# A graph network on one core: where POOL's matrix writes stand, and how deep its gathers run ahead

## The chip, the core and the metric

The kernel runs on one core of one Trainium2 chip. The metric is the device time of one execution in microseconds (us). TensorE (PE, with its weight loads as PEld), VectorE (DVE), ScalarE (ACT), GpSimd (POOL) and SyncE (SP) run their own instruction streams and meet by semaphores. POOL issues all indirect DMAs here: those that read rows of a table by a list of indices, or write elements to places that a list gives.

## The reference

The reference is a chain of eight blocks on x, 1875 nodes x 256 features, each added to x. Four have to do with the change. The first is a stack of four graph layers over 31875 edges sorted by destination:

```
e = edge_attr @ eW + eb
m = relu(x[src] + e)
agg = segment_sum(m, dst, num_segments=N)
h = (1.0 + eps) * x + agg
return relu(h @ W1 + b1) @ W2 + b2
```

with `y = relu(layernorm(h))` between layers. Then comes a feed-forward block on the half of the nodes with the highest score. The third is relational attention with 8 relations and 8 heads:

```
h_all = einsum('nf,rof->rno', x, W)
scores = einsum('ehd,hd->eh', h_all[edge_type, src], attn_src) + einsum('ehd,hd->eh', h_all[edge_type, dst], attn_dst)
scores = leaky_relu(scores);  w = exp(scores - amax[dst]);  w = w / denom[dst]
out = segment_sum(h_src * w, dst)
```

Behind it stand a switch feed-forward block, a two-layer graph convolution (which uses the edge weights as a dense matrix), a top-2 block, another convolution and a last top-2 block.

## The kernel before

The nodes are held as T = 15 tiles of 128 rows, the edges as EC = 264 chunks of 128. A loop pass handles U = 12 chunks in groups of G = 4, so there are 264 / 12 = 22 passes. The program is cut into phases; at the end of each, all engines meet in a barrier, so a phase lasts as long as its slowest engine.

**The matrix writes.** The convolutions behind the attention want the edge weights as dense adjacency matrices in HBM. `Adjacency.send(pool, count)` writes the next `count` of the 264 chunks, 128 single elements each, as one indirect DMA (L488). Nothing needs them before the first convolution, where `arrived` waits for all. So the kernel hands them to POOL in small lots in phases in which POOL has little else to do: 4 in each of four dense parts (`gine_mlp`), 6 in each of three norms between the layers, 10 in the stack's last norm, 30 in the ranking of the nodes, 6 in the attention's norm, 14 in `relation_scores`, and the remaining 170 at the start of `relation_rows`.

**The edge stage** (`gine_edges`, four times). For each chunk POOL gathers the source rows from an HBM table into one of RING = 24 buffers (`gather_rows`, L833), TensorE makes the edge term (L880, L881), VectorE adds it (L919), ScalarE applies relu (L898), TensorE sums by destination with a one-hot matrix (L890), and VectorE adds the sum to the accumulator (L927). The buffer is free when `agg_done` counts the chunk; `gather_rows` knows this semaphore as `used`.

**The norm** (`layernorm`) computes on VectorE, writes the gather table through SP, and turns the tiles on TensorE (L676) for the next stage.

**The rows stage** (`relation_rows`, phase "score"). In each pass VectorE makes 12 one-hot tiles and raises `hot_ready` after each group of four (L1992), TensorE turns them (L1930), ScalarE copies them out (L1964), TensorE picks the destination scores (L1940), and VectorE multiplies and reduces (L1999, L2003). The first T = 15 passes also compute the rows of the relation table (L1919), which ScalarE copies (L1972) and SP writes to HBM; the last 7 passes have no such products. POOL has no part in it but the matrix writes.

**The ordered attention** (`attend_in_order`, phase "inorder"). POOL gathers rows of 264 values from that table into HELD = 44 buffers (L2219). Windows of up to 11 chunks go through a chain of small operations on VectorE and TensorE (L2276 to L2299) before their messages are weighted and summed as in the edge stage.

Of the kernel before, what the change touches and what calls it, by code (L numbers as in the profile page):

```python
# [22 lines left out]
EC = 264  # L23
# [6 lines left out]
G = 4  # L30
# [795 lines left out]
def gather_rows(nc, pool, rows, table, got, gathered, used):  # L826


    for c in range(EC):

        if c >= RING:
            pool.wait_ge(used, c - RING + 1)
        pool.indirect_dma_start(got[:, c % RING, :], None, table,  # L833
                                bass.IndirectOffsetOnAxis(ap=rows[:, c:c + 1], axis=0)).then_inc(gathered[c % RING], 16)
# [96 lines left out]
def gine_mlp(nc, g, agg, h, w1, b1, w2, b2, first, stats):  # L931


    with Phase(nc, "mlp") as ph:
# [17 lines left out]
        @block.gpsimd  # L952
        def _(pool):
            g.adj.send(pool, 4)

# [55 lines left out]
def gine_stack(nc, g, i):  # L1011

    with Phase(nc, "stack") as ph:
# [3 lines left out]
        for k in range(L):  # L1017
            table = g.dram(f"gine_table{k}", [NP, D])
            affine = {} if k == 0 else dict(gamma=i["L0_gnn_gamma"][k, :], beta=i["L0_gnn_beta"][k, :], relu=True, stats=stats, edges=6)
            layernorm(nc, g, g.X if k == 0 else h, y, table=table, addrow=i["L0_gnn_eb"][k, :], turned=acc,  # L1020
# [3 lines left out]
                     i["L0_gnn_b2"][k, :], first=(k == 0), stats=stats)  # L1024
        layernorm(nc, g, h, y, gamma=i["L0_gnn_gamma"][0, :], beta=i["L0_gnn_beta"][0, :], relu=True, add=g.X, stats=stats, edges=10)

# [10 lines left out]
def rank_tokens(nc, g, xn, wr, br, chosen, r):  # L1037
# [4 lines left out]
    with Phase(nc, "rank") as ph:  # L1042
# [19 lines left out]
        @block.gpsimd  # L1062
        def _(pool):
            g.adj.send(pool, 30)

# [664 lines left out]
def relation_scores(nc, g, xt, w, attn_src, attn_dst, score_src, score_dst, o):  # L1730
# [5 lines left out]
    with Phase(nc, "rel") as ph:  # L1736
# [31 lines left out]
        def _(pool):  # L1768
            nc.gpsimd.iota(chunk[:, :], [[1, EC + PADS]], base=0, channel_multiplier=0,
                           allow_small_or_imprecise_dtypes=True).then_inc(chunk_made, 1)  # L1770
            g.adj.send(pool, 14)

# [86 lines left out]
def relation_rows(nc, g, score_src, score_dst, scores, xt, wt, h_table):  # L1859
# [4 lines left out]
    with Phase(nc, "score") as ph:  # L1864
# [35 lines left out]
        def _(pool):  # L1900
            nc.gpsimd.iota(rel_idx[:, :], [[1, R]], base=0, channel_multiplier=0,
                           allow_small_or_imprecise_dtypes=True).then_inc(iota_made, 1)
            g.adj.send(pool, 170)

# [282 lines left out]
def attend_in_order(nc, g, o, h_table, scores, acc):  # L2187
# [6 lines left out]
    with Phase(nc, "inorder") as ph:  # L2194
# [19 lines left out]
        def _(pool):  # L2214
            for c in range(EC):

                if c >= HELD:
                    pool.wait_ge(agg_done, c - HELD + 1)
                pool.indirect_dma_start(got[:, c % HELD, 0:FULL], None, h_table,  # L2219
                                        bass.IndirectOffsetOnAxis(ap=g.hrow[:, c:c + 1], axis=0)).then_inc(gathered[c % HELD], 16)  # L2220
# [146 lines left out]
def relational_attention(nc, g, i):  # L2367

    h_table = g.dram("h_table", [NP * R, FULL])
    with Phase(nc, "rgat") as ph:  # L2370
        scores, order = ph.sb("scores", [P, EC, HD]), Order(ph.sb)
        with Phase(nc, "rgat_in") as inner:
            score_src, score_dst = inner.sb("score_src", [P, T, R, HD]), inner.sb("score_dst", [P, T, R * HD])
            xt = inner.sb("xt", [P, T, 2, P])
            with Phase(nc, "rgat_ln") as first:
                xn = first.sb("xn", [P, T, D])
                layernorm(nc, g, g.X, xn, turned=xt, edges=6)
            relation_scores(nc, g, xt, i["L1_gnn_W"], i["L1_gnn_attn_src"], i["L1_gnn_attn_dst"], score_src, score_dst, order)
# [109 lines left out]
```

## Time and profile before

| | us |
|---|---|
| median of 3 runs | 4837.89 (4830.57 to 4844.03) |
| the profiled execution | 4816.76 |
| its span | 4815.1 |
| edge stages, each | 411 to 413 |
| rows stage (2349.5 to 2833.6) | 484.0 |
| ordered attention (2833.6 to 3269.6) | 436.0 |
| POOL busy, in all | 1824.1 (38%) |
| TensorE busy, in all | 2940.5 (61%) |
| VectorE busy, in all | 2290.0 (48%) |

The stage times are from the first instruction of a phase on VectorE to the next phase's. Busy shares of the whole span mix phases with different limits, so a phase is read by itself: which engines are busy in it, and what ends last. A gap between two instructions is put down to a releaser. "issue" means that the engine waited for nothing that the profile shows. Semaphore names are reused, so a releaser such as "DMA unpack_rows<-in_edge_rows" in a late phase stands for another semaphore in the same slot.

### The profile page before, as it was taken

To read this page: it belongs to the slowest core of one execution; us is meant where nothing else is said; L and a number is where in the kernel's file an instruction comes from. 1 tells how busy PE (TensorE), PEld (TensorE's weight loads), DVE (VectorE), ACT (ScalarE), POOL (GpSimd) and SP (SyncE) were. 2 spreads that over 40 slices of the span, in tenths; PEclk is the share of its full clock that TensorE was granted. 3 is DMA by queue.
4 is the path that set the end of the run, shared out by engine and by line. 5 is a ranking of instruction groups with operands and counts; after the bars stand their busy time and mean duration, and the time that the engine had idled before them with its cause. 6 is when DMAs were issued, how large, how long until landed. Compare 5 with 4: busy or idle time off the path is not lost. (4 is left out here: it accounts for less than half of the span.)

```text
span 4815.1 us, 58214 instructions
## 1 busy us (share of the span) xinstructions
PE 2940.5 (61%) x16851; PEld 2371.2 (49%) x16852; DVE 2290.0 (48%) x6653; ACT 868.0 (18%) x2228; POOL 1824.1 (38%) x1982
## 2 busy tenths in 40 slices
PE   3566756675667566606405945673949829948392
PEld 3455545554555455405304723333948729937382
DVE  7666556665665566652202436784154421134113
ACT  1122212221222222202001310000310103310020
POOL 4366446645663566342472036651010020020212
PEclk8788878887888788857557956775979959979696
DMA  6633223322332333215001213332947539945594
GB/s 163 207 90 91 69 76 89 90 62 84 90 90 53 91 90 90 48 37 181 18 1 46 89 45 89 95 71 81 335 156 240 186 103 331 327 161 171 176 334 133
DMA packets 357404, 599.03 MB, mean 124 GB/s; under 512 B 81862, under 2 KB 239864, under 8 KB 354808
## 3 DMA queue, kind: packets, MB, share of 16 engines
q1 hardware_dynamic: 245816, 357.76, 22.2%
q0 software_dynamic: 88640, 214.25, 15.6%
q10 hardware_dynamic: 22656, 23.54, 1.5%
q8 instruction: 132, 2.16, 0.2%
q14 instruction: 160, 1.31, 0.1%
HBM read 499.63 MB, written 95.75 MB: 124 GB/s over the span
## 5 line engine op out<-in xcount | busy, mean ns | idle before, releaser
L833 POOL DMA_INDIRECT gine_got<-gine_table,src x1056 | 1003.6, 950 | 672.7 <-issue 269.2
L890 PE MATMUL gine_p_sum<-gine_hot,gine_got 128*128 128x128 f32 x4224 | 843.9, 332 | 537.7 <-issue 209.6
L890 PEld LDWEIGHTS gine_p_sum<-gine_hot,gine_got 128*128 128x128 f32 x4224 | 690.3, 232 | 731.1 <-issue 622.3
L919 DVE TENSOR_TENSOR gine_got<-gine_got,gine_p_edge 128x256 f32<-128x256 f32 x1056 | 440.3, 417 | 563.2 <-PE gine_p_edge L881 336.8
L898 ACT ACTIVATE gine_got<-gine_got 128x256 f32<-128x256 f32 x1056 | 439.8, 416 | 1182.2 <-issue 690.4
L927 DVE TENSOR_TENSOR stack_acc<-stack_acc,gine_p_sum 128x256 f32 x1056 | 437.7, 415 | 3.5
L2219 POOL DMA_INDIRECT edge_space<-h_table,hrow x264 | 262.6, 995 | 386.1 <-issue 329.9
L488 POOL DMA_INDIRECT adjacency<-value,place x264 | 264.7, 1002 | 311.9 <-POOLq L54 133.9
L842 DVE TENSOR_SCALAR gine_hot<-iota_free,dst 128x128 f32<-128x128 f32 x1056 | 348.8, 330 | 60.2 <-issue 29.2
L880 PE MATMUL gine_p_edge<-gine_w_a,edge_space 128*128 128x256 bf16 x1056 | 331.7, 314 | 34.7 <-DVEq L910 17.4
L1365 PE MATMUL ffn_p_h<-ffn_xt,ffn_w 128*128 128x128 f32 x2864 | 347.5, 279 | 0.9 <-DMA ffn_w<-in_L_ffn_w 0.4
L1365 PEld LDWEIGHTS ffn_p_h<-ffn_xt,ffn_w 128*128 128x128 f32 x2864 | 337.6, 196 | 2.9 <-DMA ffn_w<-in_L_ffn_w 1.8
L1377 PE MATMUL ffn_p_y<-ffn_w,ffn_ht 128*128 128x256 f32 x1432 | 328.6, 380 | 5.4 <-DMA ffn_w<-in_L_ffn_w 5.3
L881 PE MATMUL gine_p_edge<-gine_w_b,edge_space 128*128 128x256 bf16 x1056 | 331.0, 313 | 0.0
L2254 PE MATMUL inorder_p_sum<-edge_space,inorder_hot 128*128 128x265 f32 x528 | 235.8, 562 | 133.5 <-issue 70.0
L1431 DVE TENSOR_TENSOR ffn_y<-ffn_p_y,ffn_b 128x256 f32<-128x256 f32 x112 | 47.6, 425 | 549.3 <-PE ffn_p_y L1377 549.3
L1402 ACT ACTIVATE ffn_ht<-ffn_p_h,ffn_b 128x128 f32<-128x128 f32 x716 | 204.7, 369 | 549.1 <-PE ffn_p_h L1365 549.0
L1630 PE MATMUL gcn_p_out<-gcn_h,gcn_a 128*128 128x256 f32 x1350 | 299.0, 380 | 0.0
L1377 PEld LDWEIGHTS ffn_p_y<-ffn_w,ffn_ht 128*128 128x128 f32 x1432 | 263.7, 190 | 39.2 <-DMA ffn_w<-in_L_ffn_w 7.7
L1630 PEld LDWEIGHTS gcn_p_out<-gcn_h,gcn_a 128*128 128x128 f32 x1350 | 254.2, 191 | 33.0
L2254 PEld LDWEIGHTS inorder_p_sum<-edge_space,inorder_hot 128*128 128x128 f32 x528 | 108.2, 253 | 229.6 <-issue 227.6
L1143 POOL IOTA route_e_idx<- 128x8 f32 (+1 forms) x3 | 0.4, 136 | 573.9 <-POOLq L54 573.9
(398 smaller groups left out, 3537.1 us busy)
## 6 DMA issues: line engine op xcount, KB each, us to landing
gcn_a<-adjacency SPq DMA_DIRECT2D x270, 320.0 KB
ffn_w<-in_L_ffn_W SPq DMA_DIRECT2D x74, 1024.0 KB
ffn_w<-in_L_ffn_w SPq DMA_DIRECT2D x60, 1024.0 KB
ffn_w<-in_L_ffn_w SPq DMA_DIRECT2D x90, 512.0 KB
adjacency<-zero_row ACTq DMA_DIRECT2D x3, 7200.0 KB, 43.7
gine_got<-gine_table,src POOLq DMA_INDIRECT x1056
h_table<-score_rows SPq DMA_DIRECT2D x15, 1056.0 KB
adjacency<-zero_row SPq DMA_DIRECT2D x1, 7200.0 KB, 28.1
```

The lines of the kernel that those rows point to most:

```text
L833: pool.indirect_dma_start(got[:, c % RING, :], None, table, bass.IndirectOffsetOnAxis(ap=rows[:, c:c + 1], axis=0)).then_inc(gathered[c % ...
L842: nc.vector.tensor_scalar(hot[:, c % HOTS, :], g.iota_free[:, :], g.dst[:, c:c + 1], None, ALU.is_equal).then_inc(hot_ready, 1)
L880: nc.tensor.matmul(p_edge[c % 4][:, 0:D], g.attrs_t[:, c, :], w_a[:, :], start=True, stop=False)
L881: nc.tensor.matmul(p_edge[c % 4][:, 0:D], g.attrs_t[:, c, :], w_b[:, :], start=False, stop=True).then_inc(edge_done, 1)
L890: ins = nc.tensor.matmul(p_sum[d % 4][:, half * P:(half + 1) * P], got[:, d % RING, half * P:(half + 1) * P], hot[:, d % HOTS, :], start=T ...
L898: nc.scalar.activation(got[:, c % RING, :], got[:, c % RING, :], ACT.Relu).then_inc(msg_ready, 1)
L919: nc.vector.tensor_tensor(got[:, c % RING, :], got[:, c % RING, :], p_edge[c % 4][:, 0:D], ALU.add).then_inc(summed, 1)
L927: nc.vector.tensor_tensor(a, a, p_sum[d % 4][:, 0:D], ALU.add).then_inc(added, 1)
L1365: ins = nc.tensor.matmul(p_h[n % 2][m // 4][:, m % 4, :], w1_sb[:, n % 2, k, m * P:(m + 1) * P], xt[:, n % 2, k, :], start=(k == 0), stop= ...
L1377: ins = nc.tensor.matmul(p_y[n % 2][:, 0:D], ht[:, n % 2, m, :], w2_sb[:, n % 2, m, :], start=(m == 0), stop=(m == m_all - 1))
L1630: ins = nc.tensor.matmul(p_out[d][:, 0:D], a[:, n % RA, d * P:(d + 1) * P], h[:, t, :], start=(t == 0), stop=(t == T - 1))
L2254: nc.tensor.matmul(p_sum[c % SUMS][:, 0:WIDE], hot[:, c % HOTS, :], got[:, c % HELD, :], start=True, stop=True).then_inc(agg_done, 1)
```

## The change

Three things change, all of them on POOL. The matrix writes are spread otherwise:

| phase | before | after |
|---|---|---|
| four dense parts | 4 each | 0 |
| three norms between layers | 6 each | 17 each |
| last norm of the stack | 10 | 20 |
| ranking | 30 | 45 |
| norm of the attention | 6 | 12 |
| relation scores | 14 | 4 |
| rows stage | 170 at its start | 132, two after each `hot_ready` |

In the rows stage POOL waits before each pair of writes until VectorE has finished the next group's one-hot tiles. `gather_rows` may be only `min(24, 4 + c // 2)` chunks ahead, which is 24 from chunk 40 on. And of the first 44 gathers of the ordered attention only two are in flight at a time.

```diff
@@ gather_rows
-        if c >= RING:
-            pool.wait_ge(used, c - RING + 1)
+        ahead = min(RING, 4 + c // 2)
+        if c >= ahead:
+            pool.wait_ge(used, c - ahead + 1)
         pool.indirect_dma_start(got[:, c % RING, :], None, table,
@@ gine_mlp
-            g.adj.send(pool, 4)
+            g.adj.send(pool, 0)
@@ gine_stack
-            affine = {} if k == 0 else dict(..., edges=6)
+            affine = {} if k == 0 else dict(..., edges=17)
...
-        layernorm(nc, g, h, y, ..., add=g.X, stats=stats, edges=10)
+        layernorm(nc, g, h, y, ..., add=g.X, stats=stats, edges=20)
@@ ranking
-            g.adj.send(pool, 30)
+            g.adj.send(pool, 45)
@@ relation_scores
-            g.adj.send(pool, 14)
+            g.adj.send(pool, 4)
@@ relation_rows
-            g.adj.send(pool, 170)
+            for n in range(EC // G):
+                pool.wait_ge(hot_ready, n + 1)
+                g.adj.send(pool, 2)
@@ attend_in_order
                 if c >= HELD:
                     pool.wait_ge(agg_done, c - HELD + 1)
+                elif c >= 2:
+                    pool.wait_ge(gathered[c - 2], 16)
@@ relational_attention
-                layernorm(nc, g, g.X, xn, turned=xt, edges=6)
+                layernorm(nc, g, g.X, xn, turned=xt, edges=12)
```

What this does to POOL's instruction stream is seen at three places. (The names in brackets are those of semaphores that first had the slot; a wait "for unpack6_moved1_5" is one for `agg_done` or `hot_ready` of the phase.)

The first is POOL from the second dense part through the norm into the third edge stage. Before:

```order
L952 UNCONDITIONAL_BRANCH [waits barrier_Pool_Activation_PE_DVE_SP_gather]
L488 DMA adjacency<-value,place 3720192x1 x4
L54 UNCONDITIONAL_BRANCH
L723 UNCONDITIONAL_BRANCH [waits barrier_Pool_Activation_PE_DVE_SP_gather]
L488 DMA adjacency<-value,place 3720192x1 x6
L54 UNCONDITIONAL_BRANCH
L868 UNCONDITIONAL_BRANCH [waits barrier_Pool_Activation_PE_DVE_SP_gather]
L833 DMA gine_got<-gine_table,src 128x256 x24
L833 DMA gine_got<-gine_table,src 128x256 [waits gine10_gathered11] x240
```

After:

```order
L953 UNCONDITIONAL_BRANCH [waits barrier_Pool_Activation_PE_DVE_SP_gather]
L723 UNCONDITIONAL_BRANCH [waits barrier_Pool_Activation_PE_DVE_SP_gather]
L488 DMA adjacency<-value,place 3720192x1 x17
L54 UNCONDITIONAL_BRANCH
L869 UNCONDITIONAL_BRANCH [waits barrier_Pool_Activation_PE_DVE_SP_gather]
L834 DMA gine_got<-gine_table,src 128x256 x7
L834 DMA gine_got<-gine_table,src 128x256 [waits gine10_gathered11] x257
```

The dense part's writes are gone, the norm's are 17, and of the 264 gathers 7 instead of 24 go without a wait.

The second is POOL in the rows stage. Before:

```order
L1899 UNCONDITIONAL_BRANCH [waits barrier_Pool_Activation_PE_DVE_SP_gather]
L1901 IOTA score_rel_idx 128x8
L488 DMA adjacency<-value,place 3720192x1 x170
L54 UNCONDITIONAL_BRANCH
L63 ISA [waits barrier_Pool_Activation_PE_DVE_SP_gather]
```

After, the first two pairs of 66:

```order
L1900 UNCONDITIONAL_BRANCH [waits barrier_Pool_Activation_PE_DVE_SP_gather]
L1902 IOTA score_rel_idx 128x8
L488 DMA adjacency<-value,place 3720192x1 [waits unpack6_moved1_5]
L488 DMA adjacency<-value,place 3720192x1
L488 DMA adjacency<-value,place 3720192x1 [waits unpack6_moved1_5]
L488 DMA adjacency<-value,place 3720192x1
```

Where 170 writes stood without any wait, each pair now waits for VectorE.

The third is POOL in the ordered attention. Before:

```order
L2213 UNCONDITIONAL_BRANCH
L2219 DMA edge_space<-h_table,hrow 128x264 x44
L2219 DMA edge_space<-h_table,hrow 128x264 [waits unpack6_moved2_4] x220
L54 UNCONDITIONAL_BRANCH
L2392 UNCONDITIONAL_BRANCH [waits barrier_Pool_Activation_PE_DVE_SP_gather]
```

After, with the first waits and the last of 42:

```order
L2216 UNCONDITIONAL_BRANCH
L2224 DMA edge_space<-h_table,hrow 128x264 x2
L2224 DMA edge_space<-h_table,hrow 128x264 [waits pairs7_spread]
L2224 DMA edge_space<-h_table,hrow 128x264 [waits pairs7_compared]
L2224 DMA edge_space<-h_table,hrow 128x264 [waits pairs7_summed]
...
L2224 DMA edge_space<-h_table,hrow 128x264 [waits gine10_msg_ready]
L2224 DMA edge_space<-h_table,hrow 128x264 [waits unpack6_moved2_4] x220
L54 UNCONDITIONAL_BRANCH
```

Each of gathers 2 to 43 now waits for the landing of the gather two before it.

## Rows read from the trace of the kernel before

**Rows 1.** Windows by stage: a gather stage, rank, the rows stage in two halves; columns in the first row.

```profile
core 0: us, PE busy (x) PEld busy (x) DVE busy (x) ACT busy (x) POOL busy (x), PEclk, DMA share, GB/s
645.00:1057.00 412.00, 266.49 (x1604) 210.32 (x1602) 246.19 (x804) 112.43 (x267) 251.05 (x264) 0.84 0.31 86
2064.00:2137.00 73.00, 0.40 (x1) 0.10 (x1) 54.12 (x112) 0.00 (x0) 32.05 (x30) 0.50 0.08 16
2350.00:2592.00 242.00, 35.32 (x149) 22.77 (x150) 16.15 (x41) 7.86 (x16) 165.82 (x171) 0.53 0.07 14
2592.00:2833.00 241.00, 208.37 (x1389) 159.46 (x1387) 115.68 (x381) 67.27 (x140) 0.00 (x0) 0.80 0.15 63
```

**Rows 2.** Timeline of TensorE in the rows stage (start us, us, engine, line, op [idle before <-releaser]).

```profile
2359.89 1.44 PE L1930 MATMUL score_p_hot<-ident_b,score_hot 128*128 128x128 bf16 x12 [17.52 <-issue]
...
2366.05 0.72 PE L1940 MATMUL score_p_dst<-score_parts,edge_space 128*128 x19
...
2402.58 0.59 PE L1919 MATMUL score_p_rows<-score_wt,score_x_tile 128*128 128x256 f32 x1 [2.21 <-issue]
```

**Rows 3.** Timeline of VectorE in the rows stage: two products of matmul results.

```profile
2414.51 0.42 DVE L1999 TENSOR_TENSOR score_picked<-score_p_dst,score_rel 128x256 f32<-128x256 f32 x1 [56.68 <-DMA unpack_rows<-in_edge_rows]
...
2588.97 0.42 DVE L1999 TENSOR_TENSOR score_picked<-score_p_dst,score_rel 128x256 f32<-128x256 f32 x1 [97.63 <-DMA unpack_rows<-in_edge_rows]
```

**Rows 4.** Timeline of POOL in the rows stage: its last matrix write.

```profile
2568.33 0.97 POOL L488 DMA_INDIRECT adjacency<-value,place  x1 [0.30 <-issue]
```

**Rows 5.** Timeline of VectorE at the start of the second gather stage: chunks 4 and 7.

```profile
660.96 0.42 DVE L919 TENSOR_TENSOR gine_got<-gine_got,gine_p_edge 128x256 f32<-128x256 f32 x1 [0.47 <-issue]
...
687.90 0.42 DVE L919 TENSOR_TENSOR gine_got<-gine_got,gine_p_edge 128x256 f32<-128x256 f32 x1 [10.95 <-DMA unpack_rows<-in_edge_rows]
```

**Rows 6.** Timeline of POOL in the second gather stage: gathers 0 and 28, a burst, the last.

```profile
649.94 0.98 POOL L833 DMA_INDIRECT gine_got<-gine_table,src  x1 [20.75 <-POOLq L54]
...
689.60 0.94 POOL L833 DMA_INDIRECT gine_got<-gine_table,src  x1 [3.31 <-DMA unpack_rows<-in_edge_rows]
...
881.60 0.95 POOL L833 DMA_INDIRECT gine_got<-gine_table,src  x1 [1.21 <-DMA unpack_rows<-in_edge_rows]
...
890.43 0.95 POOL L833 DMA_INDIRECT gine_got<-gine_table,src  x1 [1.62 <-DMA unpack_rows<-in_edge_rows]
...
1035.03 0.94 POOL L833 DMA_INDIRECT gine_got<-gine_table,src  x1 [0.58 <-PE gine_p_sum L890]
```

**Rows 7.** Windows of single passes of the rows loop: one with products, one without.

```profile
2604.00:2617.00 13.00, 12.29 (x82) 9.88 (x81) 5.50 (x20) 4.16 (x9) 0.00 (x0) 0.89 0.20 83
2768.00:2779.00 11.00, 7.26 (x48) 4.73 (x48) 5.76 (x19) 1.76 (x3) 0.00 (x0) 0.50 0.00 0
```

**Rows 8.** Timeline of POOL in the ordered attention: gather 11.

```profile
2852.65 0.95 POOL L2219 DMA_INDIRECT edge_space<-h_table,hrow  x1 [0.30 <-issue]
```

**Rows 9.** Timeline of VectorE in the ordered attention: a score window and two stalls.

```profile
2855.57 0.25 DVE L2276 TENSOR_TENSOR inorder_score<-rgat_scores,edge_space 128x88 f32<-128x88 f32 x1 [12.50 <-DMA edge_space<-h_table,hrow]
...
2887.61 0.16 DVE L2290 TENSOR_TENSOR inorder_carry<-inorder_p_carry,rgat_joined 96x2 f32<-96x2 f32 x1 [13.15 <-DMA gine_table<-ln_rows]
...
2910.03 0.26 DVE L2299 TENSOR_TENSOR inorder_less<-inorder_score,inorder_p_back 128x96 f32<-128x96 f32 x1 [14.61 <-remote]
```

**Rows 10.** Timeline of POOL before the third gather stage: its first gather.

```profile
1119.77 0.99 POOL L833 DMA_INDIRECT gine_got<-gine_table,src  x1 [19.81 <-POOLq L54]
```

**Rows 11.** Timeline of POOL in the final norm: the seventh matrix write of ten.

```profile
2042.97 1.54 POOL L488 DMA_INDIRECT adjacency<-value,place  x1 [0.30 <-issue]
```

**Rows 12.** Timeline of VectorE in the final norm: its last operation.

```profile
2054.25 0.96 DVE L777 SCALAR_TENSOR_TENSOR X<-stack_y,X 128x768 f32<-128x768 f32 x1
```

**Rows 13.** Timeline of TensorE in the relation scores: tiny matmuls, and what follows them.

```profile
2287.84 0.31 PE L1783 MATMUL rel_p_near<-ident,rel_spread 128*96 128x1 f32 x2
2288.01 0.31 PE L1784 MATMUL rel_p_near<-ident,rel_spread 128*96 128x1 f32 x2
...
2305.97 13.81 PE L1791 MATMUL rel_p_proj<-rel_heads,rel_w 128*128 128x16 f32 x64
```

More of the change, by code:

```diff
@@ L1018, in gine_stack @@
             table = g.dram(f"gine_table{k}", [NP, D])
-            affine = {} if k == 0 else dict(gamma=i["L0_gnn_gamma"][k, :], beta=i["L0_gnn_beta"][k, :], relu=True, stats=stats, edges=6)
+            affine = {} if k == 0 else dict(gamma=i["L0_gnn_gamma"][k, :], beta=i["L0_gnn_beta"][k, :], relu=True, stats=stats, edges=17)
             layernorm(nc, g, g.X if k == 0 else h, y, table=table, addrow=i["L0_gnn_eb"][k, :], turned=acc,
@@ L1024, in gine_stack @@
                      i["L0_gnn_b2"][k, :], first=(k == 0), stats=stats)
-        layernorm(nc, g, h, y, gamma=i["L0_gnn_gamma"][0, :], beta=i["L0_gnn_beta"][0, :], relu=True, add=g.X, stats=stats, edges=10)
+        layernorm(nc, g, h, y, gamma=i["L0_gnn_gamma"][0, :], beta=i["L0_gnn_beta"][0, :], relu=True, add=g.X, stats=stats, edges=20)
 class Routes:
```

## The prediction

> **What bounds the kernel now.** I read the windows stage by stage first [rows 1]. A gather stage of the first part, 412 us, has POOL busy 251 us in 264 indirect DMAs (264 x 0.95); with the 0.30 us gap behind each, POOL is taken for about 330 of 412 us. The stage that makes the score rows shows something else: 242 us in which TensorE does 149 matmuls while POOL does 170 writes, then 241 us in which POOL does nothing and TensorE does 1389. Two of the 22 passes of its loop end in the first half, twenty in the second.
>
> The timelines say why. The stage's first matmul starts at 2359.89, and seven microseconds of matmuls run at full pace, up to 2366.8, though POOL has been writing since the stage began [rows 2]. From there TensorE starts about one matmul in 2.8 us (0.59 busy, 2.21 idle, "issue": nothing that the profile shows holds it). VectorE idles 56.68 and 97.63 us ahead of its products of matmul results [rows 3], though the first twelve L1940 matmuls for it had been issued by 2366.8. The stall ends with POOL's last write at 2568.33 + 0.97 = 2569.3 [rows 4], and 23 us later the second pass is done. So **POOL issuing indirect DMAs back to back starves TensorE's issue and holds back its completion signals**; how it does so the trace doesn't show. A write takes POOL 0.97 us and the gap of 0.30 behind the one before it: 1.27 apart [rows 4].
>
> The same pattern, weaker, is in the gather stage. From 649.9 POOL issues without a wait; VectorE adds chunk 4 at 660.96 and is only at chunk 7 by 687.90, with 10.95 us of idle ahead of it [rows 5]. POOL, 24 buffers ahead, waits 3.31 us at 689.60; later it issues six from 881.60 on and pauses 1.62 us, 8.83 us for six chunks [rows 6].
>
> **The change part by part.** The sum is made against the profiled execution, 4816.8 us (span 4815.1); the median of the runs shown is 4837.9, 21 above it.
>
> *Rows stage.* 170 writes at once become 6 per pass: two after each `hot_ready`. hot_ready comes 1.3 us apart at the start of a pass, so the six writes go out as one burst of 6 x 1.27 = 7.6 us, and then POOL waits for the next pass. Behind POOL's new waits stand only its own later writes, and nobody waits for those before the dense stages, so none of POOL's work is on the path if a pass is longer than 7.6 us. Undisturbed, a pass with products takes about 12.5 us (PE busy 12.29 of the 13.00 us of one), one without about 11.0 [rows 7]. What a burst costs in a pass is not in the trace. Bounds: nothing, as the first 7 us of the stage ran at full pace beside POOL [rows 2]; at most the whole burst, 7.6 us. Nearest row: in the gather stage six issues and a pause take 8.83 us [rows 6], where TensorE's 266.5 us for 264 chunks [rows 1] are 1.01 each, 6.1 for six: a burst of the same length costs 2.7 us there. I take 2.6 for the 15 passes with products and 1.0 for the 7 short ones, where TensorE has slack (7.3 busy of 11 us). Start to first matmul is 10.4 us. Sum: 10.4 + 15 x (12.5 + 2.6) + 7 x (11.0 + 1.0) = 321 us for 484: **-163**. With nothing lost 10.4 + 188 + 77 = 275: -209. With 7.6 lost in each long pass and 5 in the short: 10.4 + 302 + 112 = 424: -60.
>
> *Gather stages, four of them.* `ahead` is 7 at chunk 6, grows by one for two chunks, and is 24 from chunk 40. POOL stops early, so TensorE's signals flow earlier, and the gap of VectorE from 661 to 688 should vanish. But what ends the stage is POOL: its last gather, at 1035.03 [rows 6], needs chunk 240 used, and then 22 us drain a full ring of 24. Gather 40 needs 17 chunks used, before and after. Before, gather 28 is issued at 689.60, 40 us behind the first, and twelve more at 8.83 / 6 make 57; POOL alone would need 40 x 1.25 = 50. The pauses only come earlier. I take 0; bounds from -7 (no pause up to 40) to +5 a stage.
>
> *Ordered attention.* The first 44 gathers go two in flight. Gather 11 is issued at 2852.65 [rows 8] and the score sum that needs it starts at 2855.57 [rows 9]: 2.9 us from issue to use, so two in flight give one per 1.5 us instead of 1.25: 44 x 0.25 = +11, and the second score window starts later. Against it the stalls that VectorE has there now, 13.15 and 14.61 us [rows 9], shrink. From there the ring of 44 rules as before. Net +3, bounds -30 (both stalls given back in full) to +11.
>
> *Writes moved into the normalizations.* A gine stage's norm had six writes, then POOL idled 19.81 us before the first gather at 1119.77 [rows 10]. The six had begun at 1092.3 (1100.0 less 6 x 1.28). Seventeen take 17 x 1.28 = 21.8 us, to 1114; beside VectorE operations with two SBUF inputs one takes 1.54 instead of 0.97 [rows 11], which makes about 1118, just inside the stage's end near 1119. Those writes now lie beside the norm's last transposes on TensorE (L676) too, whose signals may be late: +2 each, +6 for three; up to +8 each. The Trainium skill ("SBUF — State Buffer", section "Who interferes with whom") says that a VectorE instruction with two SBUF inputs contends with a GpSimd instruction that reads SBUF; the 1.54 beside 0.97 agrees in kind, and by the page the writes beside one-input operations stay at 0.97, which is the 1114 above.
> The final norm gets 20 for 10: it ends at 2055.2 with VectorE [rows 12]. Its seventh write ends at 2044.5 [rows 11]; thirteen more at 1.27 to 1.84, mostly the former, end at 2061 to 2068: **+9** (6 to 13), since the stage's barrier waits for POOL. Rank, 45 for 30, has 73 us, VectorE busy for most of it [rows 1], and at 32.05 / 30 + 0.30 = 1.37 the 45 need 62: 0 (uncovered, +21). The norm before the relations, 12 for 6: +2 (0 to 7.7, six writes uncovered). The four dense parts lose 4 writes each, 5 us of POOL, shorter than the 16 us before the first hole above: 0 (-1 each).
>
> *Relation scores.* 104 tiny matmuls take 2287.5 to 2305.97 = 18.4 us; at first two start every 0.17 [rows 13], which makes 8.8 for all. The first four of the fourteen writes end ahead of them all: -10, and the 13.81 us matmuls behind, too, may gain a little: **-12** (-8 to -17).
>
> Sum: -163 + 0 + 3 + 6 + 9 + 2 - 12 = **-155**: 4662 for the profiled execution, 4683 for the median.
>
> **The rivals.**
> (1) *A burst blocks a whole pass* (0.17). Twelve L1940 results took from 2366.8 to 2414.5 to reach VectorE; if every signal of a burst is held until POOL pauses, a long pass is 20 us: -60 for the stage, -52 in all, 4786; half of it, 17.5, gives 10 + 263 + 96 = 369, -115 + 8: 4731. For: the late results [rows 3]. Against: the gather stage's 8.83 us, where signals pass within bursts [rows 6], and a stall that began only after some 16 us of POOL [rows 2].
> (2) *A pass hides the burst* (0.17): -209 + 8: 4637. For: the full pace at first [rows 2]. Against: the 8.83 us [rows 6].
> (3) *The shallow rings pay* (0.15). If the 20 to 25 us that VectorE loses at the start of each gather stage are not given back, four stages give -80 and ordered attention -25 more: 4578. For: those stalls are real [rows 5, 9]. Against: POOL's 330 us of issue and its pauses remain, and the drain of a full ring.
> (4) *TensorE was never held by POOL* (0.03), the other sign. Then its 2.8 us a matmul is something of the loop itself, passes stay as they are, and the writes hang behind them: rows 484, plus 9 + 6 + 2 + 3 - 0: 4858. It decides where a pass with six writes takes over 22 us (22 x 22 = 484). Against: 149 matmuls before POOL's last write and 1389 behind it, in equal time [rows 1]. The Trainium skill's section named above says that TensorE and ScalarE never wait on anyone; by it this rival would hold, and the trace disagrees with it as far as issue and signals go.
>
> **How the numbers follow.** My forecast has 0.48: 4683, its own range 4650 to 4710. The cases around it span 4578 to 4786; leaving out the far ends of (1) and (3) gives 4590 to 4765. A measurement here tells 0.3%, 14 us, from no change. Faster by over 0.3% are all cases but (4) and part of the worst of (1): 0.96; within 0.3% 0.015; slower 0.025.
>
> **What would show it.** Rows stage: passes of even length near 15 us from the first on, POOL's writes in 22 groups of six; no idle of VectorE over 10 us. A pass of 12.5 shows (2), of 20 (1). Gather stages: 411 us again with POOL's first wait at chunk 7. Final norm 9 us longer, ended by POOL; L1783 and L1784 without holes. The prediction is wrong if a pass differs from 15 by more than 3 us, or if a gather stage moves by more than 6.

## The result, and the profile after

The changed kernel takes 4702.94 us (median of 4 runs, 4693.92 to 4704.62) against 4837.82 us (4 runs) of the kernel before: a ratio of 0.9718, 95% interval 0.9700 to 0.9736. The prediction was 4683, with a range of 4590 to 4765. The page of the changed kernel begins with its span and the busy time of each engine:

```profile
span 4701.8 us, 58214 instructions
...
PE 2962.1 (63%) x16851; PEld 2391.2 (51%) x16852; DVE 2289.9 (49%) x6653; ACT 868.4 (18%) x2228; POOL 1835.2 (39%) x1982
```

TensorE and POOL are busy for about as long as before; it is their place that changed. The same windows as in [rows 1, 7], now of the changed kernel: a gather stage, the rows stage, a pass with products and one without, the ordered attention.

```profile
core 0: us, PE busy (x) PEld busy (x) DVE busy (x) ACT busy (x) POOL busy (x), PEclk, DMA share, GB/s
650.00:1068.00 418.00, 270.88 (x1596) 214.53 (x1596) 246.85 (x804) 112.75 (x267) 252.86 (x267) 0.82 0.31 85
2384.00:2707.00 323.00, 249.48 (x1536) 188.96 (x1536) 131.52 (x422) 76.03 (x156) 127.86 (x133) 0.74 0.21 57
2420.00:2435.00 15.00, 13.56 (x81) 10.62 (x81) 5.77 (x19) 4.26 (x9) 5.82 (x6) 0.84 0.19 73
2624.00:2636.00 12.00, 7.32 (x49) 4.70 (x49) 5.76 (x19) 1.76 (x3) 3.87 (x4) 0.53 0.01 0
2707.00:3156.00 449.00, 261.16 (x734) 132.23 (x734) 296.08 (x1029) 10.87 (x53) 263.98 (x264) 0.70 0.31 80
```

The rows stage is one stretch of 323 us where [rows 1] had 242 and 241, and its 1536 matmuls are spread over all of it. The gather stage and the ordered attention are a little longer than before. Two timelines of the stage show one pass (start us, us, engine, line, op [idle before <-releaser]). First POOL, with one burst of six and the start of the next:

```profile
2407.24 0.96 POOL L488 DMA_INDIRECT adjacency<-value,place  x1 [9.36 <-DVE score_hot L1995]
...
2413.60 0.97 POOL L488 DMA_INDIRECT adjacency<-value,place  x1 [0.31 <-issue]
2421.76 0.97 POOL L488 DMA_INDIRECT adjacency<-value,place  x1 [7.19 <-DVE score_hot L1995]
```

Then VectorE in the same pass, from its first operation (L1989) to that of the next pass:

```profile
2405.87 0.26 DVE L1989 TENSOR_TENSOR score_rel<-score_rel_idx,etype 128x96 f32<-128x96 f32 x1 [0.47 <-issue]
...
2416.11 0.42 DVE L2002 TENSOR_TENSOR score_picked<-score_p_dst,score_rel 128x256 f32<-128x256 f32 x1 [7.58 <-DMA unpack_rows<-in_edge_rows]
...
2420.39 0.26 DVE L1989 TENSOR_TENSOR score_rel<-score_rel_idx,etype 128x96 f32<-128x96 f32 x1 [0.45 <-issue]
```

A pass is 14.52 us here. POOL's burst begins 1.4 us into it and ends at 2413.60 + 0.97 = 2414.57; the product of matmul results comes 1.5 us behind that, and 4.3 us later the pass is over. The idle of 56.68 and 97.63 us of [rows 3] is gone; what is left is 7.58 in this pass. The releaser in the product's row, a DMA, is the profile's guess. The 15 passes with products take 14.5 to 16.8 us, 15.1 on average, the one behind them 14.3, and the last six 12.0 to 13.2.

The two profiled executions differ by 113 us (4816.8 to 4703.4), the medians by 135. So I ran both kernels again on one chip (below); there their spans are 4813.3 and 4678.1, 135.2 apart. Stage lengths in us, counted from VectorE's arrival at the end of one stage to its arrival at the end of the next, so that the wait at a late barrier counts for the stage behind it:

| stage | before, again | after, again | difference | predicted |
|---|---|---|---|---|
| four gather stages | 1645.1 | 1653.7 | +8.6 | 0, and +6 for the norms |
| final norm with what stands behind it, rank | 105.1 | 116.1 | +11.0 | +9 |
| relation scores, with the attention norm's end | 82.3 | 80.6 | −1.7 | −12 + 2 |
| rows stage | 485.9 | 320.5 | −165.4 | −163 |
| ordered attention | 439.1 | 450.4 | +11.3 | +3 |
| sum | | | −136.2 | −155 |

Counted from barrier to barrier instead, the four gather stages moved by 0.4 us together and the norms ahead of them by 8.5, of which 5.9 are the norm before the third gather stage, whose barrier is late. The rows stage is then 485.8 and 324.3 us, the attention 439.1 and 446.5: 4 us of the attention's +11.3 are the late barrier behind the rows stage. The dense parts and all else moved by 1.0 us together. In the first pair of profiles, 113 us apart, the rows stage gave 160.5 us and the four gather stages with their norms took 27 of it back.

### The profile page after: what moved, and what is told of

Same layout as the page of the kernel before. It is cut to its first block and busy times, and to the rows that moved or that the text cites. A ratio compares the mean times of both kernels' runs of the same rounds, so it can differ in the third digit from the quotient of the medians.

```text
span 4701.8 us, 58214 instructions
## 1 busy us (share of the span) xinstructions
PE 2962.1 (63%) x16851; PEld 2391.2 (51%) x16852; DVE 2289.9 (49%) x6653; ACT 868.4 (18%) x2228; POOL 1835.2 (39%) x1982
## 5 line engine op out<-in xcount | busy, mean ns | idle before, releaser
L891 PE MATMUL gine_p_sum<-gine_hot,gine_got 128*128 128x128 f32 x4224 | 857.1, 336 | 539.2 <-ACT gine_got L899 250.8
L891 PEld LDWEIGHTS gine_p_sum<-gine_hot,gine_got 128*128 128x128 f32 x4224 | 703.3, 236 | 734.8 <-issue 641.6
L488 POOL DMA_INDIRECT adjacency<-value,place x264 | 278.9, 1056 | 478.5 <-POOLq L54 171.4
L928 DVE TENSOR_TENSOR stack_acc<-stack_acc,gine_p_sum 128x256 f32 x1056 | 440.1, 417 | 3.4
```

The lines of the kernel that those rows point to most:

```text
L891: ins = nc.tensor.matmul(p_sum[d % 4][:, half * P:(half + 1) * P], got[:, d % RING, half * P:(half + 1) * P], hot[:, d % HOTS, :], start=T ...
L928: nc.vector.tensor_tensor(a, a, p_sum[d % 4][:, 0:D], ALU.add).then_inc(added, 1)
```

## The experiments

**One part of the change at a time** (four kernels, one chip). `rows_alone` is the kernel before with only the rows stage's writes paced:

```
-            g.adj.send(pool, 170)
+            for n in range(EC // G):
+                pool.wait_ge(hot_ready, n + 1)
+                g.adj.send(pool, 3 if n < 38 else 2)
```

> The kernel before with the rows stage's 170 writes paced (three after each of the first 38 hot_ready, two after the rest) and nothing else changed. Theory (POOL's back to back writes starve TensorE in this stage alone): the rows stage falls from 484 to about 325, since a long pass takes about 15 us; passes with nine writes (11.4 us of POOL) may be longer, up to 17.5. Whole kernel 145 to 160 us below before. Rival (the gain needs the redistribution too, since 170 writes don't fit): the stage stays above 370.

`old_rings` is the changed kernel with the gather rings of the kernel before:

```
-        ahead = min(RING, 4 + c // 2)
-        if c >= ahead:
-            pool.wait_ge(used, c - ahead + 1)
+        if c >= RING:
+            pool.wait_ge(used, c - RING + 1)
```

> The changed kernel with gather_rows as before (24 ahead from the start). Theory (the shallow start costs each gather stage 5 us): the four stages return from 417, 418, 422, 417 to 411 to 413 us (the third to 416, where 5 us are a late barrier of the norm), the kernel is 20 to 22 us faster than the changed one. Rival (the 5 us come from the writes that now stand ahead of the stage): the stages keep their 417, no difference.

`old_attention` is the changed kernel with the ordered attention's gathers unpaced, and `writes_only` has both edits, so that of the change only the moved writes are left:

```
-                elif c >= 2:
-                    pool.wait_ge(gathered[c - 2], 16)
```

> The changed kernel with the ordered attention's gathers as before (44 without a wait). Theory (two in flight cost 1.55 instead of 1.25 us each and win nothing): the stage returns from 449 to 436, the kernel 13 us faster than the changed one. Rival (the stage is longer for another reason, such as its tables' place or the stage before): 449 stays.

> The changed kernel with both rings as before, so that only the matrix writes are redistributed. If the costs add: 20 to 22 and 13 us, 33 to 35 below the changed kernel, about 4668 us. If gather stages and attention hold the same loss for another reason: the changed kernel's 4703.

Measured: the kernel before took 4285.15 us on this chip (13 runs, 4276 to 4292), over 500 less than elsewhere. Against it `rows_alone` took 4299.03 (1.0033, 1.0021 to 1.0045), `old_rings` 4325.01 (1.0082, 1.0066 to 1.0099), `old_attention` 4319.31 (1.0081, 1.0064 to 1.0098) and `writes_only` 4308.61 (1.0050, 1.0033 to 1.0067). All my numbers missed, since what the change removes wasn't there: this chip didn't hold TensorE. POOL's waits in the first gather stage of `writes_only` (waited for: us in total, times, longest):

```profile
POOL gine_got L833 <- POOLq L54: 74.0, 1, 74.0
POOL gine_got L833 <- issue: 66.4, 218, 0.3
POOL gine_got L833 <- PE gine_p_sum L890: 13.7, 45, 0.3
```

No wait is over 0.3 us but the first, which is a barrier, and a gather stage takes 344 us. On the chip of the next group POOL did wait; the changed kernel there, same view:

```profile
POOL gine_got L834 <- POOLq L54: 73.6, 1, 73.6
POOL gine_got L834 <- issue: 64.9, 209, 0.7
POOL gine_got L834 <- remote: 47.5, 33, 2.1
POOL gine_got L834 <- PE gine_p_sum L891: 23.0, 21, 1.7
```

On the fast chip the rows stage took 281.2 to 298.0 us in these four kernels. `rows_alone`'s 298 and its 14 us over the kernel before put that kernel's own stage at about 284. This is inferred, no profile of it was taken there, and it may be off by 7 us either way: `rows_alone`'s profiled execution took 6 us more than its median, and 7 us of a late barrier count for its attention. One profile is a weak measure of this stage anyway: `old_rings`, `old_attention` and `writes_only` have the same code in it and took 297, 284 and 281 us. The group still prices two parts where nothing is held. Pacing the attention costs 4325.01 − 4308.61 = 16.4 us (the stage itself 401.4 against 388.5, +12.9), and the shallow rings 4319.31 − 4308.61 = 10.7 (1.3 to 2.6 a gather stage). If these add to `writes_only`, the changed kernel would take about 4336 there, 1.012 of before; that was not measured.

**Both kernels again, and no matrix write in the rows stage** (another chip). `before_again` and `after_again` are the two kernels unchanged. `rows_none` is `writes_only` with the 132 writes of the rows stage sent in rank, and `rows_iota` keeps POOL busy in the rows stage with work that makes no DMA and whose result nobody reads. Neither leaves any of the kernel's work out.

```
-            for n in range(EC // G):
-                pool.wait_ge(hot_ready, n + 1)
-                g.adj.send(pool, 2)
-            g.adj.send(pool, 45)
+            g.adj.send(pool, 45 + 132)
+            for n in range(600):              # rows_iota only
+                nc.gpsimd.iota(busy[:, :], [[1, 128]], ...)
+                pool.drain()
```

> The kernel before, unchanged, for its trace on the chip of these runs. In the last four runs the kernel before took 4285 us where it had taken 4838, and the gather stages of every variant took 343 to 350 instead of 411, with POOL never pausing. Theory A (the hold on TensorE depends on the chip or on how the program was loaded, not on the kernel): where gather stages take about 343, the rows stage with its 170 unpaced writes takes about 284; where they take 411, it takes 484. Theory B (the hold in the rows stage is its own matter): 484 beside gather stages of 343 can't be, since the whole took 4285; a rows stage over 300 would still speak for it.

> The changed kernel, unchanged. Theory A: where TensorE isn't held, the change costs its parts: matrix writes 23 us (measured: writes alone 4308.6 to 4285.2), attention pacing 13, rings 8 for four stages, so about 4330 against 4285, ratio 1.010. Where TensorE is held: ratio 0.972 as before.

> Both rings as before, the rows stage without any matrix write (its 132 go to the ranking, which grows by some 150 us; only the rows stage is read). It gives the stage's own pace. Where TensorE is held: 275 us against 320 with bursts of six, so a burst costs 2 us a pass. Where it isn't: within 3 us of the 281 that the writes-alone kernel showed.

> As the one before, but POOL runs 600 small iotas back to back in the rows stage, with no DMA (the buffer they write isn't read by anyone). Theory (it is the issue of indirect DMAs that holds TensorE): the stage is as long as without POOL work, about 275 to 281. Rival (any busy POOL holds TensorE): where the hold shows at all, the passes under the iotas take far longer than 12.5 us. Where TensorE isn't held by DMAs either, the run tells nothing.

Measured: `before_again` 4814.92 (one run; 4813.89 is the median of 7 runs of that kernel here), `after_again` 4679.58, 0.9714 (0.9698 to 0.9730), `rows_none` 4799.49 and `rows_iota` 4794.44, one run each. The windows of the rows stage, columns as above, of `before_again`:

```profile
2345.00:2830.00 485.00, 244.34 (x1536) 182.62 (x1536) 131.76 (x422) 75.27 (x156) 165.54 (x171) 0.66 0.10 38
```

of `after_again`:

```profile
2363.00:2684.00 321.00, 245.82 (x1536) 187.29 (x1536) 132.01 (x425) 75.91 (x156) 127.88 (x133) 0.74 0.24 57
```

of `rows_none`:

```profile
2538.00:2813.00 275.00, 230.46 (x1536) 177.44 (x1536) 131.60 (x422) 74.77 (x156) 0.13 (x1) 0.79 0.16 67
```

and of `rows_iota`:

```profile
2537.00:2808.00 271.00, 227.26 (x1536) 174.96 (x1536) 132.49 (x423) 74.78 (x156) 147.27 (x601) 0.80 0.17 68
```

POOL's group of lines in that window of `rows_iota` (busy us, mean ns | idle before):

```profile
L1904 POOL IOTA score_busy<- 128x128 f32 x600 | 147.2, 245 | 78.5 <-issue 2.7
```

The gather stages are 411 us here and the rows stage of the kernel before 486, as theory A had it for a chip with the hold. Without writes the stage takes 275.1 us, what my lower bound gave (275). So the burst of six costs (320.5 − 275.1) / 22 = 2.06 us a pass, where I had 2.6 and 1.0, on average 2.1. The average hides two misses that cancel. Pass by pass, `after_again` against `rows_none`, it is 2.2 us in the 15 passes with products (14.9 against 12.8) and 1.9 in the last six (12.7 against 10.8), so the price doesn't fall where TensorE has slack, as I had assumed. Six hundred operations of POOL, 226 us with their gaps, cost nothing: a busy POOL is not what holds TensorE.

**Plain DMAs, and the writes given out anew** (a third chip). `rows_plain` is `rows_none` with 170 plain DMAs of 128 numbers each issued by POOL in the rows stage, into a table that nobody reads. `rebalanced` is `writes_only` with fewer writes where a norm's barrier waits for POOL, and more in the dense parts and in the rows stage.

```
+            for n in range(170):              # rows_plain
+                pool.dma_start(scratch[n * P:(n + 1) * P, :],
+                               g.adj.value[:, n:n + 1]).then_inc(plain, 16)
+            pool.wait_ge(plain, 16 * 170)

-  dense 0, norms 17, final norm 20, rank 45, attention norm 12
+  dense 4, norms 14, final norm 12, rank 47, attention norm 6
-                g.adj.send(pool, 2)
+                g.adj.send(pool, 3 if n < 5 else 2)
```

> Rows stage with 170 plain DMAs issued by POOL back to back (128 single elements each to a scratch table) in place of indirect writes; the writes of the stage all go to the ranking. Theory (POOL's making of DMA commands holds TensorE, whichever kind): where TensorE is held, passes take tens of us while POOL issues. Rival (only the indirect form, which reads its places from SBUF, holds it): the stage takes 272 to 276 as without POOL work.

> A version put together from what the runs showed: both rings as before, six writes a pass in the rows stage (nine in the first two passes), 12 instead of 20 in the last norm of the stack, 14 instead of 17 between layers, 4 in each dense part as before, 47 in the ranking, 6 in the attention's norm, 4 in the relation scores. Where TensorE is held (gather stages near 411): rows stage 322, attention 437 instead of 450, the last norm and the one behind it about 35 instead of 46, the third gather stage without its 5 us: 26 to 30 us below the changed kernel, ratio to before about 0.966. Where it isn't (gather stages near 343): ratio 1.000 to 1.003. Rival (the pacing of the attention is needed beside the rest): no better than the changed kernel.

Measured: `rebalanced` 4662.01 us against 4815.93, 0.9689 (0.9675 to 0.9702), where I had expected 0.966. The interval touches that of the changed kernel on the other chip (0.9698 to 0.9730), so a gain over it is likely, not shown. VectorE's wait behind the final norm is back from 14.5 us to 4.5, the attention, unpaced, from 450.4 to 441.8, and the rows stage is 325.6. `rows_plain` took 4856.62, one run, with a rows stage of 332.5 us, 57 over that of `rows_none` on the other chip. The waits in 90 us of it, 2556 to 2646, while POOL issued (waited for: us in total, times, longest):

```profile
ACT score_rows L1972 <- DMA h_table<-score_rows: 47.8, 3, 17.7
PEld score_p_rows L1922 <- ACT score_rows L1975: 34.8, 5, 13.0
...
PEld score_p_dst L1943 <- issue: 2.4, 7, 0.7
```

TensorE's "issue" idle is at most 0.7 us, where [rows 2] had 2.21 before each matmul. What waits is ScalarE, 17.7 us at a time, for SyncE's table writes to land, and TensorE for ScalarE. While POOL issues 113 plain DMAs without a pause, TensorE does the 16 matmuls of a pass's table rows as fast as in `rows_none` (3.71 us both):

```profile
2536.27 60.08 POOL L1905 DMA_DIRECT2D scratch<-value  x113 [0.31 <-issue]
```

```profile
2564.89 3.71 PE L1922 MATMUL score_p_rows<-score_wt,score_x_tile 128*128 128x256 f32 x16
```

So a plain DMA issued by POOL does not hold TensorE; many small ones delay the transfers of another queue. The first matmul of the stage, too, comes 10 us later than in `rows_none`. That of the kinds of work tried only the indirect form holds TensorE stands, though the 272 to 276 us expected with it missed this second effect. Which part of an indirect DMA it is, POOL's own work for it or its reads and writes, was not told apart here.

**The size of a burst** (a fourth chip; one run each, the kernel before 4824.18). `bursts_of_twelve` is `writes_only` with `send(pool, 4)`, so the stage's writes are out after 11 passes. `bursts_of_three` gives half of the six to the end of a pass:

```
+            for i in range(EC // U):
+                for n in range(U // G):
+                    pool.wait_ge(hot_ready, i * groups + n + 1)
+                    g.adj.send(pool, 1)
+                for n in range(U // G):
+                    pool.wait_ge(picked_done, i * groups + n + 1 + groups)
+                    g.adj.send(pool, 1)
```

> Matrix writes as in the changed kernel, both rings as before, but four after each hot_ready until all are out: 12 a pass, 15.3 us of POOL, more than an undisturbed pass, for 11 passes; then 11 passes without any. Theory (TensorE gets through in the pauses, so without a pause it collapses): where TensorE is held, the first 11 passes take over 25 us each and the stage is above 400. Rival (the cost of a burst grows with the writes, 0.34 us each, as 2.06 us for six): the first passes take 12.5 + 4, at least 15.3 for POOL, and the stage is 310 to 325.

> As the one before with six writes a pass, but one after each hot_ready and one after each picked_done, so two bursts of three. Theory (signals are held through a burst, so shorter bursts hold them less): where TensorE is held, the stage falls from 320 to 285 to 305. Rival (each write costs its 0.34 us wherever it stands): 318 to 325.

Measured: `bursts_of_twelve` 4724.36 us, rows stage 380.2; `bursts_of_three` 4629.46, rows stage 283.9. POOL's first and last write of a burst in `bursts_of_twelve`:

```profile
2413.29 0.97 POOL L488 DMA_INDIRECT adjacency<-value,place  x1 [7.77 <-DVE score_hot L1994]
...
2427.32 0.97 POOL L488 DMA_INDIRECT adjacency<-value,place  x1 [0.30 <-issue]
```

and VectorE around it:

```profile
2411.92 0.26 DVE L1988 TENSOR_TENSOR score_rel<-score_rel_idx,etype 128x96 f32<-128x96 f32 x1 [0.45 <-issue]
...
2430.38 0.42 DVE L2001 TENSOR_TENSOR score_picked<-score_p_dst,score_rel 128x256 f32<-128x256 f32 x1 [15.79 <-PE score_p_dst L1942]
...
2434.64 0.26 DVE L1988 TENSOR_TENSOR score_rel<-score_rel_idx,etype 128x96 f32<-128x96 f32 x1 [0.45 <-issue]
```

The pass is 22.72 us, and it has the shape of the one with six: 1.4 us to the burst, 15.0 of burst, 2.1 from its end to the product, 4.3 behind. In `rows_none`, with no burst, the product comes by itself. A short pass:

```profile
2559.25 0.26 DVE L1985 TENSOR_TENSOR score_rel<-score_rel_idx,etype 128x96 f32<-128x96 f32 x1 [0.47 <-issue]
...
2566.34 0.43 DVE L1998 TENSOR_TENSOR score_picked<-score_p_dst,score_rel 128x256 f32<-128x256 f32 x1 [4.42 <-PE score_p_dst L1939]
...
2570.83 0.26 DVE L1985 TENSOR_TENSOR score_rel<-score_rel_idx,etype 128x96 f32<-128x96 f32 x1 [0.45 <-issue]
```

That is 7.1 us into a pass of 11.58. Of the passes with products behind the first, six have this form and eight another, 8.8 us into 13.3. A burst is free while it ends 1.5 us before that: 7.1 − 1.5 − 1.4 = 4.2 us, three writes, and 5.9 us in the longer form, four. POOL in `bursts_of_three`:

```profile
2409.78 0.97 POOL L488 DMA_INDIRECT adjacency<-value,place  x1 [1.37 <-DVE score_hot L1998]
...
2412.33 0.97 POOL L488 DMA_INDIRECT adjacency<-value,place  x1 [0.30 <-issue]
2416.24 0.97 POOL L488 DMA_INDIRECT adjacency<-value,place  x1 [2.94 <-DVE score_picked L2005]
...
2421.40 0.97 POOL L488 DMA_INDIRECT adjacency<-value,place  x1 [1.36 <-DVE score_hot L1998]
```

This pass is 11.62 us from burst to burst. The other passes with products are 11.6 and 13.3 us, as without a burst, but for four of 14.6 to 16.9, and the stage costs 0.4 us a pass over `rows_none`. The barrier behind it is 7.5 us late, though, and with the attention the cost over `rows_none` is 12 us, 0.6 a pass. My theory expected 285 to 305, and it is 283.9, by a hair outside. For twelve neither expectation held: the theory wanted over 400 and the rival 310 to 325. The mechanism fits all three sizes in the passes with products; the theory's price of a longer burst did not, since I had not taken off the time for which the product isn't due anyway. In the last six passes, without products, it does not fit. There VectorE gets its first result before the burst is over, in the first profile of the changed kernel:

```profile
2662.34 0.97 POOL L488 DMA_INDIRECT adjacency<-value,place  x1 [0.30 <-issue]
2665.02 0.96 POOL L488 DMA_INDIRECT adjacency<-value,place  x1 [1.71 <-issue]
```

```profile
2663.04 0.42 DVE L2002 TENSOR_TENSOR score_picked<-score_p_dst,score_rel 128x256 f32<-128x256 f32 x1 [4.50 <-DMA unpack_rows<-in_edge_rows]
```

Such a pass still costs 1.9 us; why stays open. `bursts_of_three` is the fastest version seen, 0.9596 of the kernel before by one run each, without an interval. With `rebalanced`'s numbers it was not tried.

## Why the prediction was right, by its own steps

**TensorE held by back-to-back indirect DMAs: right, on three of the four chips of the experiments, and in the first pair of runs.** Where it is there, `rows_none` takes 275 us for 485.9 with the same matmuls, and neither a busy POOL nor plain DMAs do it. Rival (4) is out on these chips. The Trainium skill's sentence that TensorE and ScalarE never wait on anyone ("SBUF — State Buffer", section "Who interferes with whom") speaks of SBUF's ports; taken to reach issue and signals, as the prediction took it under rival (4), it does not hold here: the 2.21 us of "issue" idle before a matmul [rows 2] are gone where POOL makes no indirect DMA. How the hold works inside the chip no run shows. One reading of the prediction was wrong: it let the stall end with POOL's last write at 2569.3. TensorE keeps to one matmul in 2.8 us for 18 us more, though by the trace no DMA of the core moves a packet between 2572 and 2590:

```profile
2587.38 0.21 PE L1940 MATMUL score_p_dst<-score_parts,edge_space 128*128 x1 [2.59 <-issue]
2588.78 1.36 PE L1940 MATMUL score_p_dst<-score_parts,edge_space 128*128 x10 [0.49 <-issue]
```

In `before_again` it is 20 us from the last write to the next product. So behind a long row the hold outlasts the issue and the transfers. The prediction's sum doesn't use that moment.

**Rows stage, −163: measured −165.4** on one chip, with 321 expected and 320.5 us measured. A pass with products was to take 15.1 and takes 14.9 on average there; one without 12.0, and takes 12.7. That the sum is so close is in part luck: the burst costs 0.4 us less than I had in a pass with products and 0.9 more in one without. And the 2.7 us that the gather stage lent gave about the right size for a cause that I had put under rival (1): in the passes with products, the first result comes only when POOL has paused. That rival erred in adding the burst to the pass; of the 7.3 us from the start of its first write to the end of its last, 4.2 to 5.9 lie in time that a pass needs before its first product. So rival (2) is half true as well, up to three writes. (`hot_ready` comes 0.8 us apart at the start of a pass, twelve tiles in 2.44 us, and not 1.3; nothing hangs on it, since two writes take 2.5.)

**Gather stages, 0 each: +8.6 for the four with their norms (0 and +6 predicted).** The first wait of POOL is at chunk 7, as I said, and the long stall of [rows 5] is shorter, though not gone: VectorE's longest in the first 50 us is 6.81 instead of 10.95, and all its idle there 31.5 instead of 37.9 us. The stage's length isn't set there. POOL at the start of the second gather stage in the first profile of the changed kernel:

```profile
666.98 0.94 POOL L834 DMA_INDIRECT gine_got<-gine_table,src  x1 [2.07 <-PE gine_p_sum L891]
...
687.14 0.95 POOL L834 DMA_INDIRECT gine_got<-gine_table,src  x1 [2.96 <-PE gine_p_sum L891]
```

The waits of 2.07 us, at gather 7, and of 2.96 us take the place of 3.31 at gather 28 [rows 6]. In `after_again` gather 40 is issued 56 to 58 us behind the first, in `before_again` 57: my 57. Stage by stage, from barrier to barrier, the shallow start moved −1.2, +1.4, +1.5 and −0.6 us against `rows_none`. So the gather stages themselves came out as predicted, and the 8.6 us are the norms', for which I had 6. In the first profile of the changed kernel the gather stages are about 5 us longer each than in that of before, the size that I had named as a miss; on one chip they are not. Whether that is the chip or the execution stays open. Rival (3) is out: the stalls at the start were not worth anything.

**Ordered attention, +3: measured +11.3.** The +11 of the pacing came in full: gather 40 is issued 62 us behind the first, before 50. The step that failed is the credit against it, that the stalls of 13.15 and 14.61 us [rows 9] would shrink. They come later instead, 92 and 114 us behind the first gather where they had come 49 and 71 behind it, and are 8.85 and 15.30 us in `after_again`; the first wait for gathers is longer, 14.85 us for 12.50:

```profile
2712.41 0.25 DVE L2281 TENSOR_TENSOR inorder_score<-rgat_scores,edge_space 128x88 f32<-128x88 f32 x1 [14.85 <-DMA edge_space<-h_table,hrow]
...
2784.81 0.26 DVE L2304 TENSOR_TENSOR inorder_less<-inorder_score,inorder_p_back 128x96 f32<-128x96 f32 x1 [8.85 <-remote]
...
2807.21 0.42 DVE L2289 TENSOR_TENSOR_SCAN inorder_upto<-rgat_same_run,inorder_p_turned 96x128 f32<-96x128 f32 x1 [15.30 <-DMA unpack_rows<-in_edge_rows]
```

VectorE's idle in the first 180 us grew from 80 to 86 us. POOL's last gather is issued 6.7 us later behind the first. The rest is a later start: 9.3 us from VectorE's last operation of the rows stage to the first gather, before 5.3. Unpaced, the stage is 440.1 in `rows_none` and 441.8 in `rebalanced`.

**Final norm, +9: measured +11 with rank.** In `after_again` VectorE is through at 2059.9 and the last write ends at 2068.8, 8.9 us behind it: the term as I had it. But the barrier comes 5.4 us behind the last write (below), which I had not in the sum. Rank, counted between the barriers, gave 4.5 us back. The two-input operations slow a write in kind as in [rows 11].

**Relation scores, −12: measured −1.7**, with the norm's end. The 104 tiny matmuls have no holes now, as expected. What failed is the pace: I took it from two rows. TensorE's group of lines in that stretch of `after_again`:

```profile
L1785 PE MATMUL rel_p_near<-ident,rel_spread 128*96 128x1 f32 x52 | 10.8, 277 | 0.0
L1784 PE MATMUL rel_p_near<-ident,rel_spread 128*96 128x1 f32 x52 | 10.7, 274 | 0.0
```

and its window, with the granted clock (0.61) third from the end:

```profile
2304.00:2320.00 16.00, 15.87 (x114) 15.40 (x113) 0.00 (x0) 2.04 (x4) 0.00 (x0) 0.61 0.01 1
```

They take 14.3 us from 2306.0 on, not 8.8: my 0.085 us each was their pace at the upper of the clock's two levels (2.4 GHz), and with 0.61 granted most run at the lower (1.2 GHz). The 4 us that the holes had cost came back, and 2.4 of them went to VectorE's wait behind the norm, 9.39 us instead of 6.96. The 13.81 us of [rows 13] stayed as they were.

On that chip the large term was right to 3 us, and the small ones, +8 expected and +29 measured, were too kind by 21. The forecast of 4683 lies 20 us under the median of the first pair. The profiles of that pair are nearer to each other than the medians, and there the largest miss is the gather stages with their norms, +27 us where I had 6.

## What to carry to other kernels

Look at the time from POOL's last indirect DMA of a row to the next result that another engine takes from TensorE. Here it is mostly 1.5 to 2.2 us behind six and twelve writes (20 behind the row of 170); then the length of the row is the cost, and it should be cut so that it ends before the next result is due. Price it as the stretch that sticks out behind the pass's own time, not as the burst. A cure for such a hold is worth what the chip at hand holds: the change gains 135 us on one chip, and on another, where nothing is held, its moved writes alone cost 23 us (`writes_only`), so time both kernels on more than one.

## What the runs showed of the hardware

**The hold is not there on every chip.** The kernel before takes 4285 us on one chip and 4814, 4816 and 4824 on three others. The parts are the rows stage (about 284, inferred, for 486), four gather stages (342 to 344 in `rows_alone` for 411) and the attention (about 389 for 439): some 520 of the 529 us. Five kernels ran without the hold on that chip and every kernel with it on the rest, so it isn't how one kernel was loaded; but each chip was used in one group of runs only, and chip and moment weren't told apart. The mean granted clock is 0.829 to 0.842 on that chip and 0.776 to 0.793 on the rest, which may be an effect of TensorE waiting less. Why the chips differ stays open.

**A barrier can be late behind indirect DMAs.** The last write, and the first gather behind the barrier, before the third gather stage in `after_again`, on POOL:

```profile
1114.32 0.97 POOL L488 DMA_INDIRECT adjacency<-value,place  x1 [0.30 <-issue]
1122.09 0.98 POOL L834 DMA_INDIRECT gine_got<-gine_table,src  x1 [6.80 <-POOLq L54]
```

and the barrier of the final norm, whose last write ends at 2068.80 (POOL's drains of line 54: duration ns min/median/max, start of the first and the last):

```profile
L54 POOLq DRAIN  x2: 53/11874/23696, 2050.5 to 2074.4; - x2
```

POOL's drain lets go 5.4 us behind the last write here, 5.9 before the third gather stage (1115.29 to 1121.19), and 8.0 at the end of the rows stage. Behind the other two norms' rows of 17 it is 1.9 us, and in the kernel before 1.4 to 1.5 us behind six writes, but 5.2 behind the four in the last dense part and 9.1 behind the 170. So the length of the row doesn't set it; what does stays open. It is a price of moving writes up to a barrier, and the trace of before had shown that it can be 9 us.
